# Low parts of the first layer's weights on VectorE instead of GpSimd, in a fused Perceiver block

## The chip, the cores and the metric

One core of one Trainium2 chip runs the whole program. The metric is the device time in microseconds of one execution; the median over several runs is compared. Engines are named as the profile names them: PE is TensorE's matmul, PEld its weight load, DVE is VectorE, ACT is ScalarE, POOL is GpSimd, SP is SyncE, which issues the loads.

## The reference, cut to what matters

Four batches of 256 latents of width 256 go through three parts, each added to the running `x`: a cross-attention to 4096 tokens with 16 heads, a causal self-attention with one head, and two layers of a block with local attention (8 heads of 64) and a gated feed-forward.

```python
x = x + xattn(ctx_1024, layernorm(x), mask, ...)     # 16 heads
x = x + attn(layernorm(x), Qw, Kw, Vw)               # softmax(Q K' / 16 + causal) V
x = x + ffn(layernorm(x), wqkv, ..., wo, ..., w1, ..., w2, ...)

# ffn, for each of 2 layers:
h = shift_token(x)                                   # second half of the width from the token before
q, k, v = split(h @ wqkv)                            # 256 -> 3 x 512
q, k = rotary(l2norm(q) * qs), rotary(l2norm(k) * ks)
x = x + local_attention(q, k, v) @ wo                # 512 -> 256
h = layernorm(shift_token(x)) * lg + lb
a, g = split(h @ w1 + b1)                            # 256 -> 2 x 682
x = x + (a * gelu(g)) @ w2 + b2                      # 682 -> 256
```

## The kernel before

**Split weights.** To keep float32 accuracy, every weight and every moving operand is held as a high part (`hi`, rounded to the fp32r type) and a low part (`lo = raw - hi`). `split_product` (lines 63 to 65) makes each product of three matmuls: hi x hi, the low part of one times hi of the other, and the reverse. A weight's `raw` tensor lies in the same memory as its `lo`, so the low part is made in place.

**First layer's weights.** `weight_pieces` cuts the layer's weights into eight pieces, in the order `wqkv0, wqkv1, wqkv2, wo, w10, w11, w12, w2`. Per partition a `wqkv` piece and `wo` are 1024 columns in one instruction; `w10` and `w11` are two blocks of 512, `w12` two of 340, and `w2` one of 1280 and one of 256 on 42 partitions: 12 instructions. SyncE loads them (`load_piece`), ScalarE copies the high part (`high_piece`, line 1090, counts `w_high` up) and GpSimd subtracts (`low_piece`, line 1099, waits for `w_high` and counts `w_split` up by 2). TensorE waits for `w_split` before the first use of each piece (`w_ready`). The second layer's pieces are made later and wholly on GpSimd (`split_piece`, lines 1109 and 1113), once SyncE has loaded them over the first layer's.

**The self-attention, batches 0 to 3.** Each engine has its steps in an order written out by hand, and a step's semaphore waits stop the whole engine. For batch b: TensorE projects q, k and v (`mid_project`, `mid_values`); ScalarE stores the high part of q and k (`mid_qk_hi`) and VectorE the low part (`mid_qk_lo`, line 1919); TensorE multiplies (`mid_scores`); VectorE adds the mask and takes the row maxima (`mid_maxima`, line 2122), then turns them into a bias of two columns with a `tensor_scalar` (line 2127); ScalarE takes exponentials (`mid_exponentials`, line 1790); TensorE transposes, VectorE stores (`mid_store_turned`), TensorE weights the values (`mid_weighted`), VectorE adds to `x` (`mid_add`, line 2143). The norm of the next stage follows on the same engines: `first_moments` (lines 2150 and 2154) on VectorE, `first_deviations` (line 1665) on ScalarE, `first_normed` (line 2160) on VectorE, after which TensorE can transpose the latents.

**The units.** The last stage runs over 8 units (2 layers x 4 batches) as a software pipeline `for T in range(0, UNITS + 3)`: unit T is projected while T-1 has its attention, T-2 its output and norm, T-3 its feed-forward. On VectorE a unit opens with the rotation (`rotate_cos`, lines 1932, 1937 and 1941, `rotate_sin`, line 1945, `rotate_sum`, line 1951, `scale_keys`, line 1958). The rotation's tables come from GpSimd: `tables(0)` (lines 1225 and 1227), which VectorE first needs in `rotate_cos(0, 0)`. GpSimd's program is: memsets, then the pieces' low parts with `tables(0)` behind `wqkv2`, then per unit the second layer's split and the low parts of the hidden values.

**SyncE.** The first layer's loads and the tables' loads are issued in one go from 683 us. The second layer's wait for TensorE's counts (`qkv_done`, `e_done`, `up_done`, `down_done`).

Of the kernel before, what the change touches and what calls it, by code (L numbers as in the profile page):

```python
# [20 lines left out]
F32 = mybir.dt.float32  # L21
# [3 lines left out]
ALU = mybir.AluOpType  # L25
# [1031 lines left out]
def weight_pieces(t, args, l):  # L1057

    wqkv = args["L0_ffn_wqkv"][l].rearrange("(k p) n -> p k n", p=P)
    w1 = args["L0_ffn_w1"][l].rearrange("(k p) n -> p k n", p=P)  # L1060
    w2 = args["L0_ffn_w2"][l]
    pieces = [(f"wqkv{w}", [([part[:, :, w * LI:(w + 1) * LI] for part in t.wqkv + t.wqkv_raw], wqkv[:, :, w * LI:(w + 1) * LI])]) for w in range(3)]
    pieces.append(("wo", [([part[:] for part in t.wo + t.wo_raw], args["L0_ffn_wo"][l].rearrange("(k p) n -> p k n", p=P))]))
    for c in range(3):
        cols = slice(c * 256, min((c + 1) * 256, HID))
        pieces.append((f"w1{c}", [([part[:, :, side * 768 + cols.start:side * 768 + cols.stop] for part in t.w1 + t.w1_raw],
                                   w1[:, :, side * HID + cols.start:side * HID + cols.stop]) for side in range(2)]))
    pieces.append(("w2", [([part[:, 0:5, :] for part in t.w2 + t.w2_raw], w2[0:5 * P, :].rearrange("(k p) n -> p k n", p=P)),
                          ([part[0:HID - 5 * P, 5, :] for part in t.w2 + t.w2_raw], w2[5 * P:HID, :])]))
    return pieces  # L1070


TABLE_LOADS, PARAM_LOADS = 3 + 2 * DEPTH, 7 * DEPTH
# [17 lines left out]
    last.then_inc(s["w_high"], 1)  # L1091


def low_piece(pool, s, piece):

    name, blocks = piece
    pool.wait_ge(s["w_high"], PIECES.index(name) + 1)
    for (hi, lo, raw), weight in blocks:
        last = pool.tensor_tensor(lo, raw, hi.bitcast(F32), ALU.subtract)
    last.then_inc(s["w_split"], 2)  # L1100


# [24 lines left out]
def latent_stage(nc, t, sems, ws, args, out):  # L1127
# [10 lines left out]
    s = {n: sems(n) for n in names}  # L1138
    s.update(ws)

    def valid(u):
        return 0 <= u < UNITS
# [17 lines left out]
    with nc.Block() as block:  # L1160
# [59 lines left out]
        def _(pool):  # L1220
# [44 lines left out]
            for part in t.xt:  # L1265
                pool.memset(part[:].bitcast(F32), 0.0)
            pool.memset(t.v[:, :, :, LDH:LDH + 1], 1.0).then_inc(s["constants_set"], 1)
            for piece in weight_pieces(t, args, 0):
                low_piece(pool, s, piece)
                if piece[0] == "wqkv2":  # L1270
                    pool.wait_ge(s["tables_loaded"], 16 * TABLE_LOADS)
                    tables(0)
            pool.wait_ge(s["params_loaded"], 16 * PARAM_LOADS)
            for T in range(-3, UNITS - 1):
                if T == 3:
# [641 lines left out]
        def _(dve):  # L1917
# [186 lines left out]
            def mid_xt_lo(b):  # L2104
                dve.wait_ge(s["mid_xt_hi"], b + 1)
                hi, lo = (x[:, :, b * L:(b + 1) * L] for x in t.mid_xt)
                low_part(lo, halves(t.turn[1]), hi).then_inc(s["mid_xt"], 1)
# [58 lines left out]
            mid_qk_lo(1, 1)  # L2166
            mid_maxima(0)
            mid_xt_lo(3)
            mid_qk_lo(2, 0)
            mid_store_turned(0)  # L2170
            mid_qk_lo(2, 1)
            mid_maxima(1)
            mid_add(0)
            first_moments(1, range(0, QT))
            mid_qk_lo(3, 0)
            mid_store_turned(1)
# [2 lines left out]
            mid_maxima(2)  # L2179
            latents_lo(0, t.g[0])  # L2180
            mid_add(1)
            first_moments(2, range(QT, 2 * QT))
            mid_maxima(3)
            mid_store_turned(2)
# [4 lines left out]
            rotate_sin(0, 0)  # L2189
            rotate_sum(0, 0)  # L2190
            scale_keys(0, 0)
            first_normed(2, range(QT, 2 * QT))
            for T in range(0, UNITS + 3):
                if valid(T - 3):
# [65 lines left out]
                    normalise(T - 1, 3)  # L2260
                if T == 0:
                    first_normed(3, range(2 * QT, TILES))
                if valid(T + 1):
                    rotate_cos(T + 1, 0)
                if valid(T - 1):
# [206 lines left out]
```

## Time and profile before

| | us |
|---|---|
| three runs | 1087.89, 1081.82, 1082.38 (median 1082.38) |
| the profiled execution, its own time | 1083.38 |
| its span in the trace | 1081.6 |
| PE busy | 1020.2 (94%) |
| PEld busy | 947.2 (88%) |
| DVE busy | 822.5 (76%) |
| ACT busy | 659.4 (61%) |
| POOL busy | 203.0 (19%) |
| mean granted TensorE clock | 0.986 |

The span is the time from the first to the last instruction on record. Busy shares are averages over three stages with different limits: the cross-attention takes the first 683 us, the self-attention and the opening of unit 0 some 50 more, the units the rest. An engine's timeline gives start and duration of each instruction, and in brackets how long the engine sat idle before it and who ended that. The chain that ended last follows the last instruction back to what released it, step by step.

### The profile page before, as it was taken

To read this page: it belongs to the slowest core of one execution; us is meant where nothing else is said; L and a number is where in the kernel's file an instruction comes from. 1 tells how busy PE (TensorE), PEld (TensorE's weight loads), DVE (VectorE), ACT (ScalarE), POOL (GpSimd) and SP (SyncE) were. 2 spreads that over 40 slices of the span, in tenths; PEclk is the share of its full clock that TensorE was granted. 3 is DMA by queue.
4 is the path that set the end of the run, shared out by engine and by line. 5 is a ranking of instruction groups with operands and counts; after the bars stand their busy time and mean duration, and the time that the engine had idled before them with its cause. 6 is when DMAs were issued, how large, how long until landed. Compare 5 with 4: busy or idle time off the path is not lost. (4 is left out here: it accounts for less than half of the span.)

```text
span 1081.6 us, 25643 instructions
## 1 busy us (share of the span) xinstructions
PE 1020.2 (94%) x8664; PEld 947.2 (88%) x8665; DVE 822.5 (76%) x3037; ACT 659.4 (61%) x1532; POOL 203.0 (19%) x260
## 2 busy tenths in 40 slices
PE   3899999999999999999999999978999999999976
PEld 3789999999999999999999998957788998989976
DVE  5897787786787786787786877679978988988642
ACT  4466566565566565566665565557667777757732
POOL 0011111111111111111111111540024212352222
PEclk9999999999999999999999998999999999999997
DMA  6000000000000000000000100600010000110001
GB/s 200 22 3 12 11 1 0 11 12 2 13 2 0 11 12 2 13 2 0 11 12 2 33 2 2 195 4 2 1 41 21 2 2 21 34 47 2 2 3 38
DMA packets 29458, 21.73 MB, mean 20 GB/s; under 512 B 13653, under 2 KB 26921, under 8 KB 29353
## 3 DMA queue, kind: packets, MB, share of 16 engines
q1 hardware_dynamic: 28368, 20.22, 6.4%
q8 instruction: 62, 1.02, 0.4%
q10 hardware_dynamic: 984, 0.13, 0.2%
q14 instruction: 44, 0.35, 0.1%
HBM read 19.23 MB, written 1.05 MB: 19 GB/s over the span
## 5 line engine op out<-in xcount | busy, mean ns | idle before, releaser
L295 PEld LDWEIGHTS pv_ps<-v,pt 128*128 128x128 f32 x1792 | 215.9, 193 | 8.8 <-issue 2.4
L295 PE MATMUL pv_ps<-v,pt 128*128 128x65 f32 x1792 | 216.3, 273 | 2.7 <-DVE o L820 1.4
L798 DVE CUSTOM_DVE_ANT_0 s_sb<-s_ps,pen,mstate 128x256 f32<-128x256 f32 (+1 forms) x512 | 199.8, 446 | 13.4 <-issue 10.5
L493 ACT ACTIVATE probs<-s_sb,mbias 128x256 f32<-128x256 f32 (+1 forms) x512 | 203.2, 470 | 0.0
L660 POOL TENSOR_TENSOR o<-o,alpha 128x260 f32<-128x260 f32 x128 | 85.6, 669 | 573.5 <-ACT alpha L487 573.5
L502 ACT ACTIVATE pt<-turn 128x512 f32<-128x512 f32 x128 | 76.3, 596 | 121.4 <-PE turn L282 107.4
L282 PE MATMUL turn<-ident,probs 128*128 128x128 f32 x896 | 123.9, 278 | 4.1 <-DVE ql L776 2.1
L282 PEld LDWEIGHTS turn<-ident,probs 128*128 128x128 f32 x896 | 98.7, 144 | 14.1 <-issue 2.6
L820 DVE TENSOR_TENSOR o<-o,pv_ps 128x260 f32<-128x260 f32 x128 | 53.9, 421 | 47.0 <-PE pv_ps L295 36.2
L271 PE MATMUL s_ps<-kh,qh 64*128 64x256 f32 (+1 forms) x512 | 79.4, 306 | 4.2 <-DVE kl L770 1.8
L770 DVE TENSOR_TENSOR kl<-proj,kh 128x512 fp32r<-128x512 f32 (+1 forms) x63 | 41.2, 654 | 51.7 <-ACT kh L480 51.4
L480 ACT ACTIVATE kh<-proj 128x512 fp32r<-128x512 f32 (+1 forms) x63 | 35.9, 571 | 69.0 <-PE proj L65 68.7
L63 PE MATMUL proj<-xt_hi,wkv_hi 128*128 128x256 f32 (+1 forms) x252 | 75.8, 301 | 0.1
L271 PE MATMUL s_ps<-kl,qh 64*128 64x256 f32 (+1 forms) x512 | 72.3, 278 | 0.0
L271 PE MATMUL s_ps<-kh,ql 64*128 64x256 f32 (+1 forms) x512 | 72.2, 278 | 0.0
L64 PE MATMUL proj<-xt_lo,wkv_hi 128*128 128x256 f32 (+1 forms) x252 | 70.9, 281 | 0.0
L65 PE MATMUL proj<-xt_hi,wkv_lo 128*128 128x256 f32 (+1 forms) x252 | 70.9, 281 | 0.0
L1236 POOL TENSOR_TENSOR late_lo<-f_hidden,late_hi 128x256 fp32r<-128x256 f32 x48 | 36.9, 777 | 171.6 <-ACT late_hi L1761 171.6
L814 DVE COPY pt<-turn 128x512 f32<-128x512 f32 x96 | 66.4, 691 | 0.0
L1720 ACT ACTIVATE f_p<-f_p,f_bias,f_q_norm 128x128 f32<-128x128 f32 (+1 forms) x128 | 62.1, 538 | 6.7 <-DVE f_bias L1981 6.6
L271 PEld LDWEIGHTS s_ps<-kh,qh 64*128 64x128 f32 x512 | 48.7, 187 | 11.8 <-issue 5.4
L63 PE MATMUL f_g<-f_xm_hi,f_w_hi 128*128 128x256 f32 x192 | 55.6, 290 | 3.2 <-issue 3.1
(367 smaller groups left out, 2737.8 us busy)
## 6 DMA issues: line engine op xcount, KB each, us to landing
raw<-in_ctx SPq DMA_DIRECT2D x24, 128.0 KB, 2.1
f_wqkv_raw<-in_L_ffn_wqkv SPq DMA_DIRECT2D x6, 512.0 KB, 5.3
wkv_raw<-in_L_xattn_Wkv SPq DMA_DIRECT2D x2, 1024.0 KB, 8.1
f_w_raw<-in_L_ffn_w SPq DMA_DIRECT2D x8, 256.0 KB, 5.1
f_w_raw<-in_L_ffn_w SPq DMA_DIRECT2D x2, 640.0 KB
wq_raw<-in_L_xattn_Wq SPq DMA_DIRECT2D x1, 1024.0 KB, 8.1
wout_raw<-in_L_xattn_Wout SPq DMA_DIRECT2D x1, 1024.0 KB, 10.3
f_wo_raw<-in_L_ffn_wo SPq DMA_DIRECT2D x2, 512.0 KB, 4.7
```

The source lines that it names most:

```text
L63: pe.matmul(out, s_hi, m_hi, start=first, stop=False)
L64: pe.matmul(out, s_hi, m_lo, start=False, stop=False)
L65: return pe.matmul(out, s_lo, m_hi, start=False, stop=last)
L271: last = pe.matmul(t.s_ps[g % 2][:, QT * o + qt, 0:width], q[rows, g, qt * P:(qt + 1) * P], k[rows, g, 0:width], start=first, stop=end)
L282: last = pe.transpose(bank[:, (at * kts + kt) * P:(at * kts + kt + 1) * P], t.probs[g % 2][:, u, kt * P:(kt + 1) * P], t.ident[:])
L295: last = pe.matmul(t.pv_ps[:, u, :], t.pt[g % 2][:, u, kt, :], t.v[:, kt, h, :], start=(kt == 0), stop=(kt == kts - 1))
L493: last = act.activation(t.probs[g % 2][:, u, 0:kts * P], t.s_sb[g % 2][:, u, 0:kts * P], ACT.Exp, bias=t.mbias[:, at:at + 1], scale=0.125)
L502: act.activation(t.pt[g % 2][:, 0:count, 0:kts, :], t.turn[0][:].rearrange("p (u k q) -> p u k q", u=count, k=kts), ACT.Copy).then_inc(s[" ...
L660: pool.tensor_tensor(t.o[:, cols, :], t.o[:, cols, :], t.alpha[:, cols].unsqueeze(2).broadcast_to([P, GU, DH + 1]), ALU.mult).then_inc(s[" ...
L798: last = dve.tensor_tensor_reduce(out=t.s_sb[g % 2][:, u, 0:width], in0=t.s_ps[g % 2][:, u, 0:width], in1=t.pen[:, 0:width], scale=1.0, sc ...
L814: dve.tensor_copy(t.pt[g % 2][:, 2:4, :, :].rearrange("p u k q -> p (u k q)"), t.turn[1][:]).then_inc(s["pt_ready"], 1)
L1720: last = act.activation(t.p[(2 * at + o) % 4][:, cols], t.p[(2 * at + o) % 4][:, cols], ACT.Exp, bias=t.bias[:, p % 2, q, o:o + 1], scale= ...
```

## The change

`low_piece` is called on VectorE (`dve`) and no more on GpSimd (`pool`). Each of the eight pieces gets a place among VectorE's steps: one among the first batches of the self-attention, seven further on, the last two in the pipeline's pass T = 0. GpSimd goes from its memsets straight to the tables. The high parts stay on ScalarE, the loads on SyncE, and the second layer's pieces on GpSimd.

```diff
-def low_piece(pool, s, piece):
+def low_piece(dve, s, piece):
     name, blocks = piece
-    pool.wait_ge(s["w_high"], PIECES.index(name) + 1)
+    dve.wait_ge(s["w_high"], PIECES.index(name) + 1)
     for (hi, lo, raw), weight in blocks:
-        last = pool.tensor_tensor(lo, raw, hi.bitcast(F32), ALU.subtract)
+        last = dve.tensor_tensor(lo, raw, hi.bitcast(F32), ALU.subtract)
     last.then_inc(s["w_split"], 2)

 @block.gpsimd
-            for piece in weight_pieces(t, args, 0):
-                low_piece(pool, s, piece)
-                if piece[0] == "wqkv2":
-                    pool.wait_ge(s["tables_loaded"], 16 * TABLE_LOADS)
-                    tables(0)
+            pool.wait_ge(s["tables_loaded"], 16 * TABLE_LOADS)
+            tables(0)

 @block.vector
             mid_maxima(0)
             mid_xt_lo(3)
+            low_piece(dve, s, ("wqkv0", first["wqkv0"]))
             mid_qk_lo(2, 0)
             mid_store_turned(0)
             mid_qk_lo(2, 1)
             mid_maxima(1)
             mid_add(0)
+            low_piece(dve, s, ("wqkv1", first["wqkv1"]))
+            low_piece(dve, s, ("wqkv2", first["wqkv2"]))
             first_moments(1, range(0, QT))
             mid_qk_lo(3, 0)
             ...
             latents_lo(0, t.g[0])
             mid_add(1)
+            low_piece(dve, s, ("wo", first["wo"]))
+            low_piece(dve, s, ("w10", first["w10"]))
             first_moments(2, range(QT, 2 * QT))
             mid_maxima(3)
             mid_store_turned(2)
             ...
             scale_keys(0, 0)
+            low_piece(dve, s, ("w11", first["w11"]))
             first_normed(2, range(QT, 2 * QT))
             for T in range(0, UNITS + 3):
                 ...
                 if T == 0:
                     first_normed(3, range(2 * QT, TILES))
+                    low_piece(dve, s, ("w12", first["w12"]))
+                    low_piece(dve, s, ("w2", first["w2"]))
                 if valid(T + 1):
                     rotate_cos(T + 1, 0)
```

## Rows read from the trace of the kernel before

**Rows 1.** Windows: us; busy us (count) of PE, PEld, DVE, ACT, POOL; clock; DMA share; GB/s.

```profile
720.00:725.00 5.00, 2.44 (x20) 2.19 (x19) 5.00 (x9) 2.68 (x7) 0.00 (x0) 1.00 0.00 0
735.00:785.00 50.00, 44.60 (x330) 37.94 (x331) 47.74 (x151) 35.74 (x79) 0.00 (x0) 0.97 0.01 1
785.00:860.00 75.00, 73.28 (x567) 65.50 (x567) 61.06 (x169) 53.41 (x105) 25.59 (x26) 1.00 0.08 23
```

**Rows 2.** Chain that ended last, 700 to 785 us: start, length, piece.

```profile
702.61 1.23 DVE f_mid_bias L2127
...
735.29 0.99 DVE raw L2160 x4
...
736.50 1.21 DVE f_sums_raw L1932
...
781.93 0.86 PE f_g L1399 x4
```

**Rows 3.** Groups by line on POOL: out<-in, shapes, count | busy us, mean ns | idle.

```profile
L1099 POOL TENSOR_TENSOR f_w_lo<-f_w_raw,f_w_hi 128x512 fp32r<-128x512 f32 (+3 forms) x8 | 10.3, 1330 | 0.0
...
L1099 POOL TENSOR_TENSOR f_wqkv_lo<-f_wqkv_raw,f_wqkv_hi 128x1024 fp32r<-128x1024 f32 x3 | 7.1, 2401 | 4.2 <-ACT f_wqkv_hi L1090 4.2
```

**Rows 4.** Timeline of POOL, 690 to 725 us.

```profile
697.98 0.45 POOL L1225 TENSOR_TENSOR f_cos<-f_rot_cos,f_scales 128x128 f32<-128x128 f32 x1
698.40 0.59 POOL L1227 TENSOR_TENSOR f_sin<-f_rot_sin,f_scales 128x64 f32<-128x64 f32 x2
...
701.44 2.37 POOL L1099 TENSOR_TENSOR f_wo_lo<-f_wo_raw,f_wo_hi 128x1024 fp32r<-128x1024 f32 x1
703.77 10.34 POOL L1099 TENSOR_TENSOR f_w_lo<-f_w_raw,f_w_hi 128x512 fp32r<-128x512 f32 x8
```

**Rows 5.** Timeline of DVE, 684 to 714 us: start, us, instruction [idle before].

```profile
688.50 0.17 DVE L2127 TENSOR_SCALAR f_mid_bias<-f_mid_mx 128x2 f32<-128x2 f32 x1
...
691.74 0.69 DVE L1919 TENSOR_TENSOR qh<-f_g,qh 128x512 fp32r<-128x512 f32 x1 [2.29 <-ACT qh L1778]
...
695.01 0.66 DVE L2127 TENSOR_SCALAR f_mid_bias<-f_mid_mx 128x2 f32<-128x2 f32 x1
...
697.46 0.25 DVE L2154 BATCH_NORM_AGGREGATE f_mv_first<-f_first_stats 128x2 f32<-128x6 f32 x2
699.49 0.69 DVE L1919 TENSOR_TENSOR ql<-f_g,ql 128x512 fp32r<-128x512 f32 x1 [1.78 <-ACT ql L1778]
700.10 0.55 DVE L2134 COPY f_pt<-f_turn 128x384 f32<-128x384 f32 x1
...
702.61 1.22 DVE L2127 TENSOR_SCALAR f_mid_bias<-f_mid_mx 128x2 f32<-128x2 f32 x1
...
708.92 0.78 DVE L2127 TENSOR_SCALAR f_mid_bias<-f_mid_mx 128x2 f32<-128x2 f32 x1
...
713.40 1.22 DVE L1932 TENSOR_REDUCE f_sums_raw<-f_sin_part 128x16 f32<-128x1024 f32 x1 [3.24 <-ACT f_sin_part L1694]
```

**Rows 6.** Groups by line on DVE, 680 to 740 us, forms apart.

```profile
L1919 DVE TENSOR_TENSOR ql<-f_g,ql 128x512 fp32r<-128x512 f32 x6 | 4.1, 684 | 3.0 <-ACT ql L1778 1.9 <-ACT ql L1712 1.1
L1937 DVE TENSOR_TENSOR f_rot<-f_qk_sb,f_cos 128x1024 f32<-128x1024 f32 x3 | 3.6, 1213 | 0.0
```

**Rows 7.** Timeline of ACT, 688 to 712 us.

```profile
689.70 1.04 ACT L1090 ACTIVATE f_wqkv_hi<-f_wqkv_raw 128x1024 fp32r<-128x1024 f32 x1
...
698.36 0.28 ACT L1665 ACTIVATE f_log_first<-f_mv_first,eps 128x2 f32<-128x2 f32 x1
```

**Rows 8.** Timeline of DVE, 818 to 830 us.

```profile
829.05 1.35 DVE L1958 TENSOR_TENSOR f_rot<-f_rot,f_k_inv 128x512 f32<-128x512 f32 x1
```

**Rows 9.** Timeline of POOL, 804 to 832 us.

```profile
826.62 3.23 POOL L1113 TENSOR_TENSOR f_wqkv_lo<-f_wqkv_raw,f_wqkv_hi 128x1024 fp32r<-128x1024 f32 x1
```

**Rows 10.** Windows around a fall of the clock: the columns of rows 1.

```profile
781.00:782.00 1.00, 0.07 (x1) 0.10 (x2) 0.97 (x6) 0.76 (x4) 0.00 (x0) 1.00 0.00 0
782.00:786.00 4.00, 4.00 (x23) 4.00 (x23) 4.00 (x7) 1.61 (x3) 0.00 (x0) 0.57 0.00 0
```

## The prediction

> **What bounds the kernel now.** Three stages follow each other: cross-attention up to about 683 us, then the self-attention (the `mid_` steps) and the pipelined units of the last stage. The change touches only the second and the opening of the third, so I read the windows of that stretch first. From 735 to 785 us VectorE is busy 47.74 of 50 us, TensorE 44.60; from 785 to 860 us it is TensorE that is full, 73.28 of 75 us [rows 1]. In the worst five microseconds ahead of that, 720 to 725, VectorE is busy for all 5.00 and TensorE for 2.44 [rows 1]. So TensorE leads after 785 us, and VectorE before it. The chain that ended last says the same for single steps: it goes through VectorE at 702.61 (the bias of the third batch), from 735.29 to 736.50 without a break (`first_normed(3)`, then the first instruction of `rotate_cos(1, 0)`), and it is handed to TensorE at 781.93 us [rows 2]. That is where this change puts work: not on an idle engine, but on the one that sets the pace of these 100 us.
>
> Second I read GpSimd, from which the work is taken. It makes the low parts in 12 instructions of line 1099, 7.1 + 2.4 + 10.3 = 19.8 us [rows 3], and is done at 703.77 + 10.34 = 714.1 us [rows 4]. No row shows a consumer waiting for them. The only harm it does on the path is another: the `tensor_scalar` of two columns on line 2127, 0.17 us at 688.50, takes 0.66, 1.22 and 0.78 us at 695.01, 702.61 and 708.92 [rows 5]. The second ends at 703.83, and GpSimd's own instruction that began at 701.44 ends at 703.81 [rows 4]. So VectorE was held until GpSimd's instruction was over. That is what the change can win.
>
> **The change part by part.** A price first. VectorE's `tensor_tensor` takes 684 ns at 512 columns and 1213 ns at 1024 [rows 6], thus 1.033 ns a column and 155 ns fixed, and the next instruction starts some 0.08 us before the end (699.49 to 700.10 at 512 columns: 0.61 [rows 5]). The first of these reads one operand from PSUM and writes fp32r, the second reads two from SBUF and writes float32; the new ones read two from SBUF and write fp32r, and I take the same price, and bound it below by the pure slope, 1.03 ns a column (0.9 us less over the twelve), and above by the full duration without overlap (1.0 us more). Per instruction: 1024 columns 1.13 us, 512 columns 0.60, 340 columns 0.43, 1280 columns 1.40, the 42-row one of 256 columns 0.34. In all 4 x 1.13 + 4 x 0.60 + 2 x 0.43 + 1.40 + 0.34 = 9.5 us more on VectorE and 19.8 less on GpSimd.
>
> wqkv0 costs nothing. It waits for ScalarE's high part, which ends at 690.74 [rows 7], and runs to about 691.9, in a gap of 2.29 us that VectorE has until 691.74 [rows 5]. The low part behind it starts 0.2 us late at most, and the path there is TensorE's, which isn't waiting. Without that cover it would cost 1.13.
>
> wqkv1 and wqkv2 come behind `mid_add(0)`. They cost 2 x 1.13 = 2.26 us. Two things take from it. The bias of batch 1 is no longer held, which frees 0.66 - 0.17 = 0.49 us [rows 5]; `mid_add(0)` behind it also needs TensorE's product, so I count about half, 0.27. And the moments behind them end at 697.71 while ScalarE takes them only at 698.36, when its own queue gets there [rows 5, 7]: 0.65 of slack. Late: 2.26 - 0.27 - 0.65 = +1.34 us. What is queued behind is `first_moments(1)`, then ScalarE's `first_deviations(1)` and both `mid_qk_hi(3, .)` behind it in order, then VectorE's low parts of q and k, which already waited 1.78 us for ScalarE at 699.49 [rows 5]; nothing there can take the delay up. The next bias, of batch 2, is freed: 1.22 to 0.17, -1.05.
>
> wo and w10 come behind `mid_add(1)`: 1.13 + 2 x 0.60 = +2.33. Behind them stand `first_moments(2)` and `mid_maxima(3)`; the bias of batch 3 is freed, 0.78 to 0.17, -0.61. VectorE then idles 3.24 us up to 713.40 [rows 5], but this gap can't be used: it ends with ScalarE's squares, and ScalarE took them in its order behind the exponentials of batch 3, which waited for that very bias. The delay goes round through ScalarE.
>
> w11, behind `scale_keys(0, 0)`: 2 x 0.60 = +1.20, ahead of `first_normed(2)` and of `rotate_cos(0, 1)`, in a stretch with no gap (5.00 of 5 us busy [rows 1]).
>
> w12 and w2, behind `first_normed(3)`: 2 x 0.43 + 1.40 + 0.34 = +2.60, between the two pieces of the chain at 735.29 and 736.50 [rows 2]. An instruction put between two that follow each other on the chain lengthens it by its whole duration.
>
> GpSimd's `tables(0)` moves up, from 697.98. Its first half there is 0.45 + 0.59 = 1.04 us [rows 4], so about 2.1 us in all. It starts once its loads have landed, and its result isn't needed before VectorE's rotation after 713.40: cost nothing, gain nothing. No transfer is moved: SyncE's issues wait for TensorE's steps, so the second layer's loads shift with TensorE, and the second layer's split on GpSimd with them.
>
> The Trainium skill (SBUF — State Buffer, section "SBUF: two separate sides") says that VectorE and GpSimd hold their shared pair of ports one at a time for whole instructions, and that a VectorE instruction with two SBUF inputs is held too when GpSimd's reads SBUF. The trace agrees: at 829.05 a 512-column one with two SBUF inputs took 1.35 us rather than 0.69 [rows 8], beside a GpSimd instruction of 3.23 us where 2.40 is usual [rows 3, 9]. By that rule `tables(0)` could also hold the new instructions. By rows alone, this is a rival below.
>
> **Sum.** 1.34 - 1.05 + 2.33 - 0.61 + 1.20 + 2.60 = 5.8 us. On the profiled execution (span 1081.6, time 1083.38) this gives a span of 1087.4 and a time of 1089.2; on the median of the three runs, 1082.38, which is 1.0 lower, 1088.2. After 785 us TensorE is 98% busy and has no slack in which to win this back, so I carry all of it to the end.
>
> **The rivals.** *The gaps swallow it* (ends faster). If VectorE's idle time before 699.49 and 713.40 (1.78 + 3.24 = 5.0 us [rows 5]) and the 50.00 - 47.74 = 2.26 us of 735 to 785 [rows 1] were slack, 7.3 us would stand against 2.26 + 2.33 + 1.20 + 2.60 = 8.4 us inserted, and the freed biases give back 0.49 + 1.05 + 0.61 = 2.15: 8.4 - 7.3 - 2.15 = -1.1, thus 1081.3. It speaks for it that the engine is nowhere full for the whole stretch; against it that each gap ends with ScalarE, which had itself waited for VectorE. It decides if more than 8.4 - 2.15 = 6.2 us of the gaps is free; half of them free gives 1082.4 + 8.4 - 3.6 - 2.15 = 1085.0. Chance 0.14.
>
> *The clock falls longer.* At 781 to 782 TensorE is busy for 0.07 us, and over the four microseconds behind it the granted clock is 0.57 [rows 10], mostly the lower of its two levels (1.2 of 2.4 GHz). That is 4 x 0.43 = 1.7 us of work lost. With some 5 us more of waiting in TensorE between 700 and 740, such a fall can come there once or twice: +1.7 each, 1090 to 1092. Against it: between 720 and 725 TensorE is busy for only 2.44 us and the clock stays at 1.00 [rows 1]. It can also go the other way: the fall at 782 may vanish and give 1.7 back, 1086.5. Chance 0.2 for longer, 0.07 for gone.
>
> *GpSimd and VectorE hold each other.* If `tables(0)` runs while wqkv1 and wqkv2 are made, VectorE is held for up to its 2.1 us, at worst in full on top of the sum: 1090.3. That such holding exists, the 1.35 us for 0.69 shows [rows 6, 8]. Against it: the tables are loaded early, and GpSimd is free for them from 687 us. Chance 0.05.
>
> **How the numbers follow.** Forecast as summed 0.54, gaps 0.14, clock 0.2 and 0.07, holding 0.05. The bounds of the price are 5.8 - 0.9 and 5.8 + 1.0, thus 1087.3 to 1089.2 for the likeliest alone. The range takes in half of the gaps and the fall of the clock twice, and a little for the scatter of single runs: 1083.5 to 1092.5. Faster than 1071.6 (by over 1%, about what a measurement of this kernel can tell from no change) would need 11 us, five times the 2.15 us that all the freed biases give: 0.02. Slower than 1093.2 needs three falls of the clock, or a wait that I don't see, on top of the sum: 0.08. Within 1%: 0.90.
>
> **What would show it.** Line 1099 on VectorE in 12 instructions of 9.5 us, with about 1.2 us for 1024 columns; the bias of line 2127 (three lines further up in the changed kernel) at 0.17 us four times; `first_moments(1)` on ScalarE's side 1.3 us late and the first `rotate_cos` 2.0 us late, at 715.4; w12 and w2 ahead of a `rotate_cos(1, 0)` at about 742.3 instead of 736.5; TensorE's turn of 781.93 at about 787.7. If rotate_cos(0, 0) is late by much less than 2 us, the gap before 713.40 was slack and the first rival holds. If the lag of 5.8 us is there at 742 but not at 788, the steps between had slack that the chain doesn't show. If it is there at 788 and not at the end, TensorE's 98% isn't the bound I take it for, and the prediction is wrong in its last step.

## The result, and the profile after

The changed kernel took 1089.19 us in the median of 9 runs (1086.41 to 1089.91), the kernel before, on the same chip, 1086.63 us (9 runs, 1081.82 to 1087.89). The ratio is 1.0032, with a 95% interval of 1.0016 to 1.0048: 0.3% slower, 3.5 us by the ratio. The profiled execution took 1089.06 us, its span is 1087.2 us, 5.6 us longer than the span of before.

The forecast was 1088.2 us with a range of 1083.5 to 1092.5, made from a lag of 5.8 us on one profiled execution. Between the two profiled executions that lag is there (5.6 us); over many runs only some 3 us of it (2.6 between the medians, 3.5 by the ratio). Both halves of that sentence need an explanation, and the second was not foreseen. A second profile of the changed kernel, taken later, has a span of 1084.8 us, only 3.2 us longer than the span of before, so the agreement of 5.6 with 5.8 is partly luck.

The page of the changed kernel, its busy times: VectorE has 6.9 us more than before (822.5 us), GpSimd 20.0 less (203.0).

```profile
PE 1021.1 (94%) x8664; PEld 947.4 (87%) x8665; DVE 829.4 (76%) x3049; ACT 659.7 (61%) x1532; POOL 183.0 (17%) x248
```

The groups of line 1099 on DVE in the changed kernel, 680 to 760 us, forms apart (to hold against [rows 6] for the price, and against [rows 3] for what GpSimd took):

```profile
L1099 DVE TENSOR_TENSOR f_wqkv_lo<-f_wqkv_raw,f_wqkv_hi 128x1024 fp32r<-128x1024 f32 x3 | 3.6, 1219 | 1.4 <-ACT f_wqkv_hi L1090 1.4
L1099 DVE TENSOR_TENSOR f_w_lo<-f_w_raw,f_w_hi 128x512 fp32r<-128x512 f32 x4 | 2.6, 684 | 0.0
L1099 DVE TENSOR_TENSOR f_w_lo<-f_w_raw,f_w_hi 128x1280 fp32r<-128x1280 f32 x1 | 1.5, 1480 | 0.0
L1099 DVE TENSOR_TENSOR f_wo_lo<-f_wo_raw,f_wo_hi 128x1024 fp32r<-128x1024 f32 x1 | 1.2, 1217 | 0.0
L1099 DVE TENSOR_TENSOR f_w_lo<-f_w_raw,f_w_hi 128x340 fp32r<-128x340 f32 x2 | 0.9, 502 | 0.0
L1099 DVE TENSOR_TENSOR f_w_lo<-f_w_raw,f_w_hi 42x256 fp32r<-42x256 f32 x1 | 0.4, 409 | 0.0
```

The 684 ns at 512 columns are those of [rows 6] to the nanosecond, and 1024 columns differ by 6 ns. The timeline of DVE in the changed kernel, 695 to 746 us, at the places where the change put work (start, us, instruction, idle before; compare [rows 5] and the chain in [rows 2]):

```profile
695.18 0.17 DVE L2124 TENSOR_SCALAR f_mid_bias<-f_mid_mx 128x2 f32<-128x2 f32 x1
...
696.54 2.35 DVE L1099 TENSOR_TENSOR f_wqkv_lo<-f_wqkv_raw,f_wqkv_hi 128x1024 fp32r<-128x1024 f32 x2
...
699.58 0.25 DVE L2151 BATCH_NORM_AGGREGATE f_mv_first<-f_first_stats 128x2 f32<-128x6 f32 x2
...
704.18 0.17 DVE L2124 TENSOR_SCALAR f_mid_bias<-f_mid_mx 128x2 f32<-128x2 f32 x1
...
711.64 0.17 DVE L2124 TENSOR_SCALAR f_mid_bias<-f_mid_mx 128x2 f32<-128x2 f32 x1
...
715.13 1.22 DVE L1929 TENSOR_REDUCE f_sums_raw<-f_sin_part 128x16 f32<-128x1024 f32 x1 [2.85 <-ACT f_sin_part L1691]
...
740.85 2.66 DVE L1099 TENSOR_TENSOR f_w_lo<-f_w_raw,f_w_hi 128x340 fp32r<-128x340 f32 x4
743.44 1.20 DVE L1929 TENSOR_REDUCE f_sums_raw<-f_sin_part 128x16 f32<-128x1024 f32 x1
```

The bias takes 0.17 us each time instead of 0.66, 1.22 and 0.78 [rows 5]. The two instructions that follow each other on the chain of before, at 735.29 and 736.50 [rows 2], now have 2.66 us of low parts between them. Line 1929 is `rotate_cos` (1932 of before); it begins 1.7 us later than before for the first unit, and 6.9 us later for the second (743.44 against 736.50).

On ACT and POOL, the two steps on which the forecast leant besides, in the timelines of those engines in the changed kernel: ScalarE's `first_deviations(1)` now waits for VectorE and begins at 699.93 (698.36 in [rows 7]), and the tables are made before VectorE begins with wqkv1.

```profile
699.93 0.30 ACT L1662 ACTIVATE f_log_first<-f_mv_first,eps 128x2 f32<-128x2 f32 x1 [1.29 <-DVE f_mv_first L2151]
```

```profile
693.53 0.47 POOL L1225 TENSOR_TENSOR f_cos<-f_rot_cos,f_scales 128x128 f32<-128x128 f32 x1 [6.67 <-DMA f_window<-in_window]
...
694.92 0.60 POOL L1227 TENSOR_TENSOR f_sin<-f_rot_sin,f_scales 128x64 f32<-128x64 f32 x2
```

**Where 1.4 us more came in.** The chain of the changed kernel, 728 to 731 us, and the same three pieces in the kernel before (start, length, piece; a line number of before is three higher here):

```profile
728.24 1.22 PE f_pv L1435 x2
729.46 0.85 PE f_pv L1436 x2
730.31 0.85 PE f_pv L1437 x2
```

```profile
725.30 0.70 PE f_pv L1438 x2
726.00 0.43 PE f_pv L1439 x2
726.43 0.43 PE f_pv L1440 x2
```

The same six matmuls take 2.92 us instead of 1.56. Ahead of them TensorE had stood idle, as its timeline in the changed kernel says, and the windows behind it show the lower clock (the columns of [rows 1]):

```profile
728.24 1.22 PE L1435 MATMUL f_pv<-f_o,f_pt 128*128 128x256 f32 x2 [3.98 <-DVE f_pt L2131]
```

```profile
725.00:730.00 5.00, 1.76 (x4) 1.48 (x5) 4.39 (x8) 1.28 (x4) 0.00 (x0) 0.77 0.00 0
730.00:735.00 5.00, 3.98 (x22) 3.06 (x21) 3.36 (x6) 1.78 (x4) 0.00 (x0) 0.89 0.00 0
735.00:785.00 50.00, 45.09 (x328) 37.29 (x326) 46.88 (x154) 32.77 (x71) 0.00 (x0) 0.97 0.01 1
782.00:786.00 4.00, 3.21 (x33) 2.85 (x32) 3.66 (x22) 3.57 (x10) 0.00 (x0) 1.00 0.02 1
```

Before, these windows at 725 and 730 us had a clock of 1.00, while at 782 to 786 the granted clock was 0.57 [rows 10]; now it is 1.00 there. The 0.97 of the row 735 to 785 is a further fall: from 745 to 755 us the granted clock is 0.83 in the changed kernel, 1.00 in the kernel before. So in this stretch two falls came and one went.

### The profile page after: what moved, and what is told of

It reads as the page before. It is cut to its first block and busy times, and to the rows that moved or that the text cites. A ratio compares the mean times of both kernels' runs of the same rounds, so it can differ in the third digit from the quotient of the medians.

```text
span 1087.2 us, 25643 instructions
## 1 busy us (share of the span) xinstructions
PE 1021.1 (94%) x8664; PEld 947.4 (87%) x8665; DVE 829.4 (76%) x3049; ACT 659.7 (61%) x1532; POOL 183.0 (17%) x248
## 6 DMA issues: line engine op xcount, KB each, us to landing
wout_raw<-in_L_xattn_Wout SPq DMA_DIRECT2D x1, 1024.0 KB, 10.2
```

## Experiments: what the moved work costs

Below, times inside a kernel are counted from the first instruction of the self-attention's norm (683.10 us in the trace of before, 683.27 after), which leaves out what happened earlier. Five kernels take parts of the change, or of what it was meant to cure, by themselves. Four of them ran on one chip; the kernel before took 1086.57 us there (33 runs). The fifth ran on another, and its base stands with it.

**One column at a time.** What the change wins, if VectorE's bias is held by GpSimd, can be had with GpSimd left as it was. On the kernel before:

```diff
-                dve.tensor_scalar(t.mid_bias[:, QT * b:QT * b + QT], t.mid_mx[:, QT * b:QT * b + QT], -1.0 / 16.0, None, ALU.mult
-                                  ).then_inc(s["mid_bias"], 1)
+                for at in range(QT * b, QT * b + QT):
+                    last = dve.tensor_scalar(t.mid_bias[:, at:at + 1], t.mid_mx[:, at:at + 1], -1.0 / 16.0, None, ALU.mult)
+                last.then_inc(s["mid_bias"], 1)
```

> The kernel before, with one edit on VectorE: the bias of mid_maxima is made by two tensor_scalar instructions of one column each in place of one of two columns. GpSimd keeps all low parts. It isolates the gain that I counted for the change. Theory of the sum: only a form that takes GpSimd's ports is held by it; with one column it is not, so the four biases take 0.2 to 0.3 us each as at 688.5 us, and the path loses the 0.27 + 1.05 + 0.61 = 1.9 us of the held biases less about 0.1 us for each second instruction: 1.5 us faster than before, ratio 0.9986. Rival 1: any VectorE instruction with an SBUF source is held, whatever its columns: the biases still take up to 1.2 us, ratio 1.000. Rival 2: the biases are freed but their time is slack: line durations near 0.2 us and the first rotate_cos still at 713.4, ratio 1.000.

Measured: 1083.04 us, ratio 0.9973 [0.9956, 0.9990]; span 1081.9. The timeline of its DVE has the bias like this, in two instructions together, beside GpSimd's instructions that are as they were:

```profile
704.37 0.22 DVE L2128 TENSOR_SCALAR f_mid_bias<-f_mid_mx 128x1 f32<-128x1 f32 x2
```

So the holding of the bias is real and is worth some 3 us over many runs, with no part of the change in it. But this kernel's own profile is no shorter than that of before (span 1081.9 against 1081.6). That was the first sign that the profile of before might not be a typical one: in the profile of this kernel something else had taken the gain back (the table further below says what).

**Later places for w11, w12 and w2.** On the changed kernel: w11 and w12 at pass T = 2 ahead of the first `gate`, w2 at T = 2 ahead of the last one.

```diff
-            low_piece(dve, s, ("w11", first["w11"]))
             first_normed(2, range(QT, 2 * QT))
             ...
+                if T == 2:
+                    low_piece(dve, s, ("w11", first["w11"]))
+                    low_piece(dve, s, ("w12", first["w12"]))
                 if valid(T - 2):
                     gate(T - 2, 0, t.g[0])
             ...
-                    low_piece(dve, s, ("w12", first["w12"]))
-                    low_piece(dve, s, ("w2", first["w2"]))
             ...
+                if T == 2:
+                    low_piece(dve, s, ("w2", first["w2"]))
                 if valid(T - 2):
                     gate(T - 2, 2, t.g[2])
```

> The changed kernel, with w11 and w12 moved from their places to pass T = 2 behind normalise(1, 2), where VectorE waited 1.90 and 0.83 us for ScalarE in the kernel before, and w2 to the end of pass T = 2 ahead of gate(0, 2), where it waited 1.80 us. Same 12 instructions on VectorE. Theory of the sum: the 1.20 us of w11 and the 2.60 us of w12 and w2 were on the path because VectorE leads up to 785 us; behind that TensorE leads and they are hidden. So 3.8 us less than the changed kernel: what is left over before is 1.34 - 1.05 + 2.33 - 0.61 = 2.0 us or a little less, ratio to before 1.000 to 1.002. The fall of the clock at 725 to 732 us in the changed kernel comes from the sum of the delays and should go or shrink. Rival, gaps: their place does not matter, ratio stays at 1.003. Rival, clock: the time follows the number of falls of the granted clock and not the delays: the ratio moves by more or less than 3.8 us as the falls move.

Measured: 1089.48 us, 1.0037 [1.0019, 1.0055]; span 1087.7. The second unit's `rotate_cos` came 3.9 us earlier (56.26 us into the stage instead of 60.17), as it should, since 1.20 + 2.60 us were gone from that stretch. The end came no earlier.

One expectation failed ahead of that: the fall of the clock at 725 to 732 us was to go or shrink, and it didn't. With w11 gone TensorE stands idle for 2.77 us ahead of the same matmuls, just as long as in the kernel before, where no fall follows, and the clock falls all the same (PE's timeline and a window of this kernel):

```profile
726.44 0.71 PE L1435 MATMUL f_pv<-f_o,f_pt 128*128 128x256 f32 x2 [2.77 <-DVE f_pt L2131]
```

```profile
725.00:730.00 5.00, 3.56 (x13) 3.04 (x14) 3.47 (x7) 0.72 (x2) 0.00 (x0) 0.70 0.00 0
```

Of the 3.9 us, 2.2 were gone by the third unit's `rotate_cos` (765.69 us), behind another fall of the clock (0.57 from 750 to 758 us, 0.90 in the changed kernel). POOL's and DVE's timelines of this kernel say what gave back the rest:

```profile
812.01 2.34 POOL L1113 TENSOR_TENSOR f_wqkv_lo<-f_wqkv_raw,f_wqkv_hi 128x1024 fp32r<-128x1024 f32 x1 [3.54 <-DVE f_w_lo L1099]
```

```profile
815.15 0.48 DVE L2074 SCALAR_TENSOR_TENSOR f_hidden<-f_g,f_b,f_gelu 128x256 f32<-128x256 f32 x1 [3.22 <-POOL late_lo L1236]
```

`w_split` is one counted semaphore for all pieces. GpSimd's first piece of the second layer waits for all of the first layer's pieces to be counted, so with w2 late GpSimd stood still, its low parts of the hidden values were late, and VectorE waited 3.22 us for them. A wait of my own making, and a result on the place, not on the change.

**The same, with w2 earlier.** w2 at T = 2 behind the second `gate` and ahead of `maxima(T, 0)`, otherwise as above; the kernel before took 1084.93 us on this chip (23 runs).

```diff
                     gate(T - 2, 1, t.g[1])
+                if T == 2:
+                    low_piece(dve, s, ("w2", first["w2"]))
                 if valid(T):
                     maxima(T, 0)
```

> The changed kernel with w11 and w12 in pass T = 2 ahead of gate(0, 0) and w2 behind gate(0, 1), so that the second layer's split on GpSimd, which waits for the count that w2 raises (it waited 3.54 us for it with w2 at the end of the pass), finds it there. Theory: the 3.8 us of w11, w12 and w2 lie on the path only while VectorE leads; here they cost at most 1 us and the wait of 3.54 us is gone: 3 us less than the changed kernel, ratio to before 0.9995 to 1.001. Rival, gaps or slack elsewhere: as the changed kernel, 1.003, because the pieces delay maxima(2, 0) by 1.7 us and that is on the path there too.

Measured: 1086.53 us, 1.0013 [0.9998, 1.0028]; span 1086.6. That is less than the changed kernel loses (1.0025 to 1.0032), but the intervals overlap. In the trace the first unit's `normed` reaches TensorE 102.21 us into the stage instead of 105.57, 3.4 earlier, and the second's at 147.36 instead of 147.62. Most was given back in between, part of it perhaps by a fall of the clock that the changed kernel doesn't have, here in its windows:

```profile
780.00:784.00 4.00, 2.75 (x21) 2.19 (x20) 3.93 (x16) 3.88 (x11) 0.00 (x0) 1.00 0.02 1
784.00:788.00 4.00, 3.09 (x17) 3.12 (x17) 3.97 (x11) 2.11 (x7) 0.00 (x0) 0.65 0.00 0
```

4 x 0.35 = 1.4 us is what this fall can take. The places of w11, w12 and w2 matter up to here; how much at the end stays open between nothing and 3 us.

**w12 and w2 back on GpSimd.** On the changed kernel, GpSimd makes the last two pieces once VectorE has made the other six:

```diff
             tables(0)
+            pool.wait_ge(s["w_split"], 12)
+            low_piece(pool, s, ("w12", first["w12"]))
+            low_piece(pool, s, ("w2", first["w2"]))
             ...
-                    low_piece(dve, s, ("w12", first["w12"]))
-                    low_piece(dve, s, ("w2", first["w2"]))
```

> The changed kernel, with w12 and w2 back on GpSimd once VectorE has made the other six pieces. VectorE does 2.60 us less, GpSimd 4.9 us more, beside the rotation of the first unit. Theory of the sum: 2.6 us less than the changed kernel at the second unit's first rotate_cos. Rival, holding: GpSimd's instructions (up to 2.94 us for 1280 columns) now run beside VectorE instructions of two SBUF inputs (rotate_cos, rotate_sin, rotate_sum), which are held until GpSimd's is over: some of them take 2 to 3 us in place of 1.2, and of the 2.6 us at most 1 is won, or it is slower than the changed kernel.

Measured: 1092.31 us, 1.0049 [1.0033, 1.0065]; span 1091.1, the worst of all. Its timelines of POOL and DVE:

```profile
722.52 6.43 POOL L1099 TENSOR_TENSOR f_w_lo<-f_w_raw,f_w_hi 128x340 fp32r<-128x340 f32 x4 [27.66 <-DVE f_w_lo L1099]
```

```profile
722.35 1.34 DVE L2160 TENSOR_SCALAR raw<-x,f_mv_first,f_rstd 128x256 f32<-128x256 f32 x2
723.61 1.21 DVE L1932 TENSOR_REDUCE f_sums_raw<-f_sin_part 128x16 f32<-128x1024 f32 x1
724.74 3.63 DVE L1937 TENSOR_TENSOR f_rot<-f_qk_sb,f_cos 128x1024 f32<-128x1024 f32 x1
728.30 0.69 DVE L1941 TENSOR_SCALAR f_sums<-f_sums_raw 128x16 f32<-128x16 f32 x1
```

The wait let GpSimd begin just as VectorE came to `first_normed(2)` (line 2160) and the next rotation. Line 1937 took 3.63 us where 1.21 is usual [rows 6], line 1941 0.69 for 0.17, line 2160 1.34 for 0.73: some 3.6 us of holding in three places, to save 2.66 us on VectorE. The fall of the clock is longer here too: the mean granted clock of this profile is 0.978, the lowest of all. Of the three only line 1937 has two tensor inputs in SBUF. Its row is the holding of an instruction with two SBUF inputs that the Trainium skill's rule (SBUF — State Buffer, section "SBUF: two separate sides") foresees, this time to triple its length. The third rival was wrong here for its place (the tables were done at 695.5) but right in its mechanism.

**Bias and edge.** The one-column bias, and the 1x1 edge of the unit's norm without its second SBUF tensor:

```diff
-                dve.scalar_tensor_tensor(out=t.edge[:], in0=t.mv[0:1, 0, 0:1], scalar=-1.0, in1=t.mv[0:1, 0, 1:2], op0=ALU.mult, op1=ALU.mult
-                                         ).then_inc(s["edge_row"], 1)
+                dve.tensor_scalar(t.edge[:], t.mv[0:1, 0, 0:1], -1.0, t.mv[0:1, 0, 1:2], ALU.mult, ALU.mult
+                                  ).then_inc(s["edge_row"], 1)
```

> The kernel before with the one-column bias and one more edit: the edge value of a unit (a 1x1 scalar_tensor_tensor with two SBUF inputs, 2.35 us at 819.04 us, held by the second layer's split on GpSimd, 0.15 us elsewhere) becomes a tensor_scalar with one SBUF input and one column. Theory: a VectorE instruction that needs no port of GpSimd is not held: the edge takes 0.15 us, and as its wait is a piece of the chain (1.95 us at 819.38), another 1.9 us go: 3.4 us faster than before, ratio 0.997. Rival 1: the wait at 819 us is passed to the next instruction (rotate_sin has two SBUF inputs): the edge is short, the next ones are held, ratio as with the bias alone, 0.9986. Rival 2: TensorE leads there and the gain is slack: 0.9986 too, but with the next ones not held.

Measured: 1081.39 us, 0.9957 [0.9938, 0.9976]; span 1079.6. Where the edge of one unit took 2.35 us before, in the trace of before, DVE's timeline now has:

```profile
817.70 0.20 DVE L2036 TENSOR_SCALAR f_edge<-f_mv 1x1 f32<-1x1 f32 x1
817.83 0.67 DVE L1919 TENSOR_TENSOR wq_hi<-f_g,wq_hi 128x512 fp32r<-128x512 f32 x1
818.43 2.78 DVE L1945 TENSOR_TENSOR f_sin_part<-f_qk_sb,f_sin 128x512 f32<-128x512 f32 x2
```

The holding moved to the next instruction with two SBUF inputs: line 1945 takes 2.78 us where 1.28 is usual, while GpSimd's low part (817.65, 2.41 us) runs. Of the 2.15 us won at the edge, 1.50 were lost there. The biases passed theirs on as well: the first `rotate_cos` begins 1.95 us earlier into the stage than in the kernel before, but with GpSimd still at its low parts line 1937 takes 1.95 us (711.15) and line 1941 0.69 (713.03), where 1.22 and 0.17 were taken before. That gives 1.25 of the 1.95 us back.

## Experiments: which kernel before?

**A mixture.** All that seemed to help, in one: one-column bias and edge, wqkv0 alone on VectorE (its place cost nothing), the rest on GpSimd, w12 and w2 there only once VectorE has stored the second low part of unit 2's heads (the tenth count of `c_ready`; GpSimd takes up w12 at 788.59 us). On the kernel with bias and edge:

```diff
             for piece in weight_pieces(t, args, 0):
+                if piece[0] == "wqkv0":
+                    pool.wait_ge(s["w_split"], 2)
+                    continue
+                if piece[0] == "w12":
+                    pool.wait_ge(s["c_ready"], 10)
                 low_piece(pool, s, piece)
             ...
             mid_xt_lo(3)
+            low_piece(dve, s, ("wqkv0", first["wqkv0"]))
```

> The kernel before with the one-column bias and edge, wqkv0 made by VectorE in its gap before the low part of q of batch 2 (as in the changed kernel), and w12 and w2 left on GpSimd but only once unit 2's second head piece is stored, at about 786 us, when VectorE is no longer the bound. With the one-column bias alone (and edge) GpSimd's low parts still ran into the first rotation: the 1024-column product of rotate_cos took 1.95 us and the scaling behind it 0.69 in place of 1.21 and 0.17. Theory of the holding: those 1.3 us are freed too, since GpSimd is done before 710 us; the rotation of unit 0 starts 1.9 us earlier than before and stays so at rotate_cos(0, 1), and no instruction between 684 and 785 us is held. 1.0 to 1.5 us faster than bias and edge alone, ratio to before 0.994 to 0.995. Rival, slack: nothing more is won, ratio 0.996. Rival, late holding: w12 and w2 beside the VectorE work of 786 to 793 us hold it by about 1 us and give it all back.

Measured: 1082.71 us in the median of 12 runs, one of which took 1974.39 us (1081.31 without it); 0.9974 [0.9957, 0.9992]; span 1082.3. It was expected at 0.994 to 0.995, and is no better than bias and edge alone (0.9957; the intervals touch). In its DVE timeline stands an instruction that I had not counted in any sum:

```profile
700.24 3.34 DVE L2166 TENSOR_SCALAR raw<-x,f_mv_first,f_rstd 128x256 f32<-128x256 f32 x2
```

This is `first_normed(1)`. In the trace of before it took 0.73 us.

**The kernel before, unchanged, profiled twice more.**

> The kernel before, unchanged, for a second profiled execution: its 33 runs lie between 1082.2 and 1091.5 us. Theory of the clock: the same instructions at the same distances, and the granted clock falls at other places or for longer; the span differs from 1081.6 by what the falls cost. Rival: something else (loads, GpSimd's spans) differs and the clock's falls are the same.

> The kernel before, unchanged, for a third profiled execution, as the one above: the theory of the clock expects the places of the falls to vary and the held instructions of line 2127 (0.66, 1.22 and 0.78 us) to be as they were.

Measured: 1089.54 us (span 1087.7) and 1088.16 us (span 1086.3), longer than every one of the first three runs. Both expectations failed: it is not the clock alone that differs, for the instructions don't lie at the same distances, and the last two biases take 1.06 and 2.08 us in the first of the two, not 1.22 and 0.78. From the POOL and DVE timelines, first of the profile that the prediction was made from, then of each of these two:

```profile
700.56 0.73 DVE L2160 TENSOR_SCALAR raw<-x,f_mv_first,f_rstd 128x256 f32<-128x256 f32 x2
```

```profile
699.14 0.46 POOL L1225 TENSOR_TENSOR f_cos<-f_rot_cos,f_scales 128x128 f32<-128x128 f32 x1 [0.75 <-issue]
...
700.12 2.46 POOL L1099 TENSOR_TENSOR f_wo_lo<-f_wo_raw,f_wo_hi 128x1024 fp32r<-128x1024 f32 x1
```

```profile
699.95 2.78 DVE L2160 TENSOR_SCALAR raw<-x,f_mv_first,f_rstd 128x256 f32<-128x256 f32 x2
```

```profile
700.37 2.38 POOL L1099 TENSOR_TENSOR f_wo_lo<-f_wo_raw,f_wo_hi 128x1024 fp32r<-128x1024 f32 x1
```

```profile
700.44 3.72 DVE L2160 TENSOR_SCALAR raw<-x,f_mv_first,f_rstd 128x256 f32<-128x256 f32 x2
```

It is a race. `first_normed(1)`, at about 700 us, and GpSimd's low part of wo, at about 700 us too, come together. VectorE's instruction begins 17.5 us into the stage in all three profiles; GpSimd's begins at 18.3, 17.6 and 17.4. In the profile of before GpSimd had idled 1.32 us ahead of its second table and began wo only at 701.44 [rows 4], after VectorE was through. In the other two it idled 0.75 and 0.51 us and began at 700.12 and 700.37. Each row of line 2160 is two instructions (x2). In the first of these profiles the first of the two was through in 0.40 us and the second was held, 2.46 us long, until wo was done at 702.58. In the other profile both were held: the first, 2.45 us long, until wo was done at about 702.75, the second, 1.35 us long, by GpSimd's next piece, until 704.16. What follows is TensorE without latents, and in both profiles a clock that falls (in the second at 705 us); PE's timeline and windows in the first of them:

```profile
702.88 0.85 PE L1308 MATMUL f_g<-ident,raw 128*128 128x128 f32 x4 [1.96 <-DVE raw L2160]
```

```profile
702.00:704.00 2.00, 1.12 (x6) 1.06 (x7) 2.00 (x6) 0.19 (x1) 2.00 (x3) 0.79 0.48 59
704.00:706.00 2.00, 2.00 (x7) 1.63 (x5) 1.08 (x3) 0.85 (x3) 2.00 (x2) 0.50 0.15 9
```

The first `rotate_cos` then comes 33.5 and 34.4 us into the stage instead of 30.3. With the profiles of this study, those of the two kernels with a wait (below) among them, the two kinds of holding can be put in a table (first `rotate_cos`, us into the stage):

| | `first_normed(1)` not held | held |
|---|---|---|
| bias held | 30.30 (before), 30.28 (before, wo waits) | 33.47, 34.41 (before, again) |
| bias in single columns | 28.35 (bias and edge), 28.34 (mixture, wo waits) | 30.38 (one column), 30.95 (mixture) |

The held `first_normed(1)` costs 3.2 to 4.1 us in the kernel before, with the falls of the clock behind it in the figure; the held biases cost 1.9 us without it and 3 or more with it.

**One wait takes the race away.** On the kernel before, GpSimd begins wo only once `first_normed(1)` is done:

```diff
             for piece in weight_pieces(t, args, 0):
+                if piece[0] == "wo":
+                    pool.wait_ge(s["y_ready"], 2)
                 low_piece(pool, s, piece)
```

> The kernel before with one wait more on GpSimd: ahead of wo's low part it waits until VectorE has made first_normed(1) (two tensor_scalar of 256 columns). Nothing is taken off GpSimd. In two further profiled executions of the kernel before these two instructions took 2.78 and 3.72 us, because GpSimd's instruction of 2.4 us had begun just ahead of them; in the one that the prediction was made on they took 0.73. Theory of the race: with the wait they always take 0.73 us, TensorE's turn of the latents is not late, and its clock does not fall at 702 to 708 us: the times gather near 1082 to 1083 us, ratio to before 0.997. Rival: what spreads the runs of before is the clock alone, whose falls come from elsewhere: median 1085 to 1086 and the same spread, ratio 1.000.

The same wait in the mixture:

> The hybrid (one-column bias and edge, wqkv0 on VectorE in its gap, w12 and w2 late on GpSimd) with that same wait ahead of wo. In its profiled execution first_normed(1) was held for 2.6 us (3.34 us in place of 0.73) and the clock fell at 724 to 728 us. Theory of the holding: now no VectorE instruction of the self-attention and of unit 0 is held; the first rotate_cos starts 28.4 us after the stage's start (30.3 in before's first profile, 33.5 and 34.4 in the two others, 31.9 in the changed kernel), the second 7.2 us behind it. Times 1078 to 1081 us, ratio to before 0.993 to 0.995, faster than both kernels. Rival: the clock falls more often as soon as VectorE is shorter, and the ratio stays at 0.997 as without the wait.

And the changed kernel once more, beside them on the same chip:

> The changed kernel, unchanged, for a second trace and against before on the same chip as the other two. No instruction of VectorE between 684 and 785 us is held, so its distances up to the first rotate_cos are those of its first profile (31.9 us from the stage's start, within 0.2), and what differs is where the clock falls; ratio to before 1.002 to 1.005.

Measured, the kernel before at 1087.97 us (29 runs, 1082.02 to 1091.05) on this chip:

| | us | highest | ratio |
|---|---|---|---|
| before, wo waits | 1083.85 (12 runs) | 1086.72 | 0.9973 [0.9955, 0.9991] |
| mixture, wo waits | 1080.62 (12 runs) | 1084.44 | 0.9946 [0.9925, 0.9967] |
| the changed kernel | 1089.77 (10 runs) | 1091.47 | 1.0025 [1.0006, 1.0044] |

In the DVE and POOL timelines of the kernel before with the wait:

```profile
699.85 0.73 DVE L2162 TENSOR_SCALAR raw<-x,f_mv_first,f_rstd 128x256 f32<-128x256 f32 x2
```

```profile
700.71 2.37 POOL L1099 TENSOR_TENSOR f_wo_lo<-f_wo_raw,f_wo_hi 128x1024 fp32r<-128x1024 f32 x1 [0.68 <-issue]
```

The wait costs GpSimd 0.68 us and holds nobody. Up to the last `rotate_cos`, 300 us into the stage, each one in this profile begins within 0.1 us of where it does in the first profile of before. Of the 29 runs of the kernel before 18 lie above 1086.72 us, the highest of this one, while the lowest times differ by only 0.5 us: it is the long executions that are gone. The rival, the clock alone, wanted 1085 to 1086 us and an unchanged spread; but a spread of 5.2 us stays, for which the race is no reason. And against this kernel, which is the one the profile of before had shown, the change costs 1089.77 - 1083.85 = 5.9 us (by the two ratios 1.0025 / 0.9973, thus 0.52%, 5.7 us), where 5.8 was forecast. The two sets of runs hardly touch (highest with the wait 1086.72, lowest of the changed kernel 1086.66), but the intervals leave some 3 us either way. The second profile of the changed kernel begins its first `rotate_cos` 31.87 us into the stage, as forecast (31.86 in the first). The mixture with the wait is faster than both kernels: 7.4 us below the kernel before in the medians (5.9 by the ratio), 9.2 below the changed one; its first `rotate_cos` came at 28.34 us, as expected.

## Why the prediction was right, and where it wasn't

**The price of the low parts: right.** 9.5 us were forecast for what VectorE gains in work; the group rows come to 10.2 us of durations, and with the 0.08 us of overlap the blocks took 2.35 (wqkv1 and wqkv2; forecast 2.26), 1.22 + 1.29 - 0.09 = 2.42 (wo and w10; 2.33), 1.29 (w11; 1.20) and 2.66 (w12 and w2; 2.60). Each is a full duration at its last instruction, of which the next one takes 0.08 back. The type and place of the operands made no difference.

**wqkv0 in the gap: right.** It ran at 691.02, and the low part behind it began at 692.16, 0.42 us later than the 691.74 of [rows 5]; 0.17 of that is the later begin of the stage, and 0.2 were forecast. Nothing behind it shows a delay by it.

**wqkv1 and wqkv2: +1.34 forecast, +1.4 measured** at ScalarE's `first_deviations(1)` (698.36 to 699.93, less the 0.17 us by which the stage began later). The slack of 0.65 us in ScalarE's queue was there, and is used up: ScalarE now waits 1.29 us for VectorE.

**First `rotate_cos`: 2.0 us late forecast, 1.6 measured** (31.86 against 30.30 us into the stage). At the end of the last bias the lag is still 1.9 (711.81 against 709.70, less 0.17). Then the gap ahead of `rotate_cos` shrinks from 3.24 to 2.85 us: the prediction had said that this gap can't be used, and 0.4 us of it were. The first rival, that the gaps swallow the work, got these 0.4 us of the 5.0 it counted on.

**Up to the second `rotate_cos`: +5.8 forecast, +6.8 measured.** With the 0.4 us of the step above taken off, the sum stands at +5.4; the other 1.4 us are the six slower matmuls at 728 us, behind a fall of the clock. The prediction had argued against such a fall from the window 720 to 725 of [rows 1], where TensorE was half idle at a clock of 1.00. The "clock falls longer" rival happened. Why it fell stays open: TensorE had idled 3.98 us for VectorE's `f_pt`, but with later places for w11, w12 and w2 it idled 2.77 us there, as in the kernel before, and the clock fell too. So w11, which made the gap longer, is not needed for the fall, and the length of this one gap doesn't decide it.

**From there to the end: +6.7 us at TensorE's turn** (105.57 us into the stage against 98.83), **+5.5 at the last matmul** (400.93 against 395.41). The fall at 745 to 755 us cost nothing on this way. The prediction carried all of its lag to the end, and most of it was carried: in both profiles of the changed kernel each `rotate_cos` from 131 to 256 us into the stage is 5.2 to 5.5 us late, the last one (983.29 us before, 987.85 and 987.95 after) 4.4 and 4.6. What was given back up to 131 us is about the size of the fall at 782 to 786 us, 4 x 0.43 = 1.7 us, that is gone. So the rival "the fall vanishes" seems to have happened as well, and the two nearly cancel: +1.4 and -1.7. But at the last matmul the second profile is only 3.2 us late (398.65 us into the stage), where the first is 5.5; from 1035 us on its granted clock is 0.90, in the first profile 0.86. The 5.8 us is right as a sum; the clock's part in it is right by luck, and so is the close agreement at the end of the first profile.

**The tables: right.** They were made from 693.53 to 695.5, and wqkv1 began at 696.54. GpSimd waited for their loads until 693.53; had these landed some 2 us later, tables and wqkv1 would have run side by side, which no run shows.

**The step that failed** is the one behind the sum, its base: "on the median of the three runs, 1082.38, which is 1.0 lower, 1088.2". It took one profiled execution and three runs for the kernel. The profile, by its row, was of the lucky kind, and two of those runs, by their times, probably too; over 9 runs of the same kernel the median is 1086.63 and over 29 on another chip 1087.97. The prediction named three held biases as the only harm done by GpSimd's low parts. There was a fourth place, `first_normed(1)` at 700.56 (the first of the timelines shown with the repeats), 0.73 us long, with GpSimd's low part of wo 0.15 us behind its end (701.44 in [rows 4], against 701.29). The change frees that one too, always. With it at 3.2 to 4.1 us in a part of the executions, 5.8 becomes some 3 us. What share it is, the runs don't say, since only profiled executions show the instruction: it was held in 2 of 3 profiles of the kernel before, and in 2 of the 3 kernels that had GpSimd make wo with no wait ahead of it and single columns (one column; bias and edge; mixture). The time of 1088.2 was close to the 1089.2 measured, but for the comparison with before the prediction was too high: 5.8 us against 2.6 to 3.5.

## What to carry to other kernels

Before costing a change at one place, look through the trace for pairs of instructions on VectorE and GpSimd that pass each other by some tenths of a microsecond: in this kernel such a pair came out differently from one execution to the next, and one profile shows one outcome. If the helper engine's work has slack, one wait that orders the pair is cheaper than moving the work to the busy engine (here 0.27% won by a wait against 0.25% lost by moving, both against the kernel before). And where pieces are counted on one semaphore, moving the last of them delays every waiter for the total, not only those who need it.

## What was not expected of the hardware

- A VectorE `tensor_scalar` on two columns behind GpSimd's low parts took up to 1.22 us in the profile of before [rows 5] and 2.08 in the repeats, for 0.17. On one column it was never held: 0.21 to 0.22 us for the pair in each of the four kernels that had it, 11 of the 16 pairs beside a running GpSimd instruction. A 1x1 edge took 2.35 us as `scalar_tensor_tensor` with two SBUF tensors and 0.20 as `tensor_scalar` with a scalar operand.
- Freeing one instruction need not remove the holding; it can go on to the next one (1.50 of 2.15 us at the edge, 1.25 of the 1.95 us of the biases in the same kernel).
- The idle time that decides the race is GpSimd's own, between two instructions of `tables(0)` with nothing to wait for in the record: 1.32, 0.75 and 0.51 us in the three profiles of the kernel before, 0.69, 1.31 and 0.72 with single columns, with bias and edge, and with the wait. Why it varies stays open.
- Falls of TensorE's clock come and go with delays of a few microseconds, and behind the same idle time of 2.77 us there was a fall in one kernel and none in another. The mean granted clock was 0.986 in the profile of before, 0.981 and 0.986 in its repeats, 0.985 and 0.987 in the two profiles of the changed kernel; 0.001 of it is 1.1 us over the span, if TensorE leads throughout. Between equal kernels that is up to 5 us as an estimate, though not all of it lies on the path: the repeats differ by 0.005 and their spans by 1.4 us, the two profiles of the changed kernel by 0.002 and 2.4 us. A sum from one trace can't be trusted to better than a few microseconds.
